# A four-layer graph network on one core: the s2 row sent round through memory, the layer-one slope on VectorE, the mask's diagonal in place, and a new order of the steps

## The reference, cut to what matters

```python
# layer 0
Wh = x @ W.T;  s1 = Wh @ a1;  s2 = Wh @ a2
e  = leaky_relu(s1[:, :, None] + s2[:, None, :], 0.2)
x  = layernorm(x + softmax(where(adj == 0, -inf, e)) @ Wh)
# layer 1
e  = leaky_relu(Ax.T + Ay + (h @ a_12) @ h.T, 0.2)
e  = where(adj > 0, e, -9e15)
x  = layernorm(x + elu(x @ W_1 + softmax(e) @ x @ W_2))
# layer 2: four heads, mask = adj | eye
x  = layernorm(x + relu(softmax(where(mask, q @ k.T * scale, min)) @ v @ Wo + bo))
# layer 3: relational convolution; with a 0/1 adj only relation 1 (the loop weights) is there
x  = layernorm(x + relu(onehot(adj.T == 1) @ ((h + b) * sigmoid(g + bg))))
```

## Time and profile before

| | |
|---|---|
| median of 3 runs | 497.16 us (495.63 to 498.61) |
| the profiled execution | 496.9 us, of which the span of the instructions is 495.0 us |
| mean granted TensorE clock | 0.988 of full speed |
| busy share PE, DVE, ACT, POOL | 95%, 83%, 86%, 75% |
| DMA | 26.93 MB, 54 GB/s in the mean |

### The profile page before, as it was taken

The page is one execution under the profiler, slowest core; times in us unless marked ns, Lnnn a source line. Parts: engine busy times, 40 slices in busy tenths (PEclk is TensorE's granted clock), DMA queues, the critical chain, the costliest instruction groups (busy, mean ns, idle before and its releaser), DMA issues. The chain is left out here.

```text
span 495.0 us, 13988 instructions
## 1 busy us (share of the span) xinstructions
PE 468.4 (95%) x3872; PEld 402.3 (81%) x3872; DVE 410.8 (83%) x1605; ACT 428.0 (86%) x1261; POOL 370.6 (75%) x736
## 2 busy tenths in 40 slices
PE   6968999999999999999999999999999999999793
PEld 5756778988888888988888888888888888877572
DVE  5657898998888998898888988898898989876653
ACT  3558999999999999999999999999999999988750
...
DMA packets 40222, 26.93 MB, mean 54 GB/s; under 512 B 2641, under 2 KB 39889, under 8 KB 40146
## 3 DMA queue, kind: packets, MB, share of 16 engines
...
...
## 5 line engine op out<-in xcount | busy, mean ns | idle before, releaser
L1211 POOL TENSOR_SCALAR x<-y,minus_mean,rstd 128x128 f32<-128x128 f32 x244 | 144.8, 601 | 6.8 <-issue 5.1
L788 ACT ACTIVATE p<-p,nmax 128x256 f32<-128x256 f32 x256 | 128.5, 530 | 0.4 <-DVE nmax L981 0.4
L981 DVE CUSTOM_DVE_ANT_0 p<-ps,neg 128x256 f32<-128x256 f32 x256 | 90.7, 420 | 2.3 <-PE ps L564 2.3
L1193 POOL TENSOR_TENSOR rstd<-ve,minus_half 128x2 f32<-128x2 f32 x128 | 91.1, 712 | 0.0
L575 PE MATMUL ps<-ident,p 128*128 128x128 f32 x512 | 78.0, 275 | 4.1 <-DVE nmax L981 3.4
L1186 POOL TENSOR_SCALAR ve<-stats 128x2 f32<-128x2 f32 x128 | 24.6, 192 | 72.3 <-DVE stats L896 64.9
L797 ACT COPY p2T<-ps 128x512 f32<-128x512 f32 x128 | 75.2, 590 | 1.3 <-PE ps L575 0.5
L575 PEld LDWEIGHTS ps<-ident,p 128*128 128x128 f32 x512 | 61.3, 143 | 9.3 <-DVE nmax L981 4.0
L788 ACT ACTIVATION_READ_ACCUMULATOR p<-p,nmax 128x1 f32 x256 | 56.1, 219 | 0.0
L896 DVE BATCH_NORM_STATS2 stats<-y 128x6 f32<-128x256 f32 x128 | 54.1, 423 | 1.5
L1175 POOL TENSOR_TENSOR relu<-relu,neg 128x512 f32<-128x512 f32 x32 | 37.1, 1161 | 21.1 <-ACT relu L757 21.1
(11 more groups left out here) (130 smaller groups left out, 1210.3 us busy)
## 6 DMA issues: line engine op xcount, KB each, us to landing
adj_in<-in_adj_dram SPq DMA_DIRECT2D x32, 256.0 KB, 3.0
xT<-in_xT_dram SPq DMA_DIRECT2D x32, 128.0 KB, 2.1
x_in<-in_x_dram SPq DMA_DIRECT2D x32, 128.0 KB, 2.1
x_aside<-x SPq DMA_DIRECT2D x32, 128.0 KB, 2.1
out_dram<-x SPq DMA_DIRECT2D x32, 128.0 KB, 2.9
...
l_w<-in_l_w_dram SPq DMA_DIRECT2D x1, 256.0 KB
...
```

What stands on the lines that cost most here:

```text
L788: last = nc.scalar.activation(p2(n)[:, k, a, :], p2(n)[:, k, a, :], ACT.Exp, bias=nmax2(n)[:, k, a:a + 1], scale=-1.0, accum_out=sum2(n)[: ...
L981: last = nc.vector.tensor_tensor_reduce(p2(n)[:, k, a, :], bank("sc2", n, a)[:, k * N:(k + 1) * N], neg2(n)[:, k, :], -1.0, HIGHEST, ALU.a ...
L1193: nc.gpsimd.tensor_tensor(rstd[layer](n), ve[layer](n), minus_half[:, :], ALU.pow)\
L1211: last = nc.gpsimd.tensor_scalar(dst[:, k, 0:D], y_t[layer](n)[:, k, :], minus_mean[layer](n)[:, k:k + 1], rstd[layer](n)[:, k:k + 1], ALU ...
```

## The change

- `first_w` gets a third column, so that `proj0` gives 0.8 s1, s2 and 0.2 s2 (131 columns per half).
- For graphs 3 to 31 `s2_rows` and `c_s2` are dropped. Instead SP writes the columns s2 and 0.2 s2 of `xw0` to memory (`s2_out`) and, once that has landed, reads them back as one row broadcast to all partitions (`s2_in`), into an `s2row` of 256 pairs. `e0` reads both of its operands from it, with a step of two elements. Graphs 0 to 2 go the old way.
- In layer 1 `relu1` becomes a copy scaled by 0.2, a new step `lk1` on DVE takes max(z, 0.2 z) over all 512 columns in one instruction, and `e1` reads its result and `neg1` from SBUF. `rmask1` on POOL is gone. The bank of `z1` is given back by `lk1`.
- `neg2` multiplies only the two 128 x 128 diagonal blocks of `neg0` in place, after `m0`; `e2a` and `e2b` read `neg0`, whose ring grows from 3 to 7, and `neg2`'s own ring is gone.
- Rings: `xw0` 3 to 4, `s2row` 2 to 3, `x4` 2 to 3. Two signals of the norm are merged into one semaphore.
- All places of `PLAN` are new; the flag steps go behind everything else.

```diff
 PLAN = {
-    "sync": [("ld_xT", 6707), ("ld_adj", 7906), ("ld_w", 8043), ("ld_x", 8602), ("aside", 16291), ("store", 19013)],
-    "tensor": [("proj0", 8774), ("s2_rows", 9402), ("prep_a", 11038), ("pT0", 11053), ("prep_c", 11151),
-        ("agg0", 11161), ("prep_d", 11846), ("prep_b", 12046), ("xT1", 12143), ("tT", 12198), ("z1", 12448),
-        ("xw1", 12450), ("pT1", 12863), ("flag", 13095), ("agg1", 13150), ("xT2", 13535), ("qk2", 13667),
-        ("sc2", 13818), ("pT2b0", 14335), ("pT2a0", 14520), ("pT2a1", 14582), ("rs_rows", 15014), ("v2", 15091),
-        ("pT2b1", 15180), ("agg2", 15365), ("wo2", 15578), ("xT3", 16401), ("hg3", 16731), ("agg3", 17296)],
...
+    "sync": [("ld_xT", 6855), ("s2_out", 8238), ("ld_adj", 8269), ("s2_in", 8279), ("ld_w", 8302), ("ld_x", 8425),
+        ("aside", 18831), ("store", 19788)],
+    "tensor": [("proj0", 7766), ("s2_rows", 8633), ("prep_a", 10144), ("pT0", 10921), ("agg0", 11174),
+        ("prep_c", 11246), ("prep_b", 11419), ("prep_d", 11635), ("xT1", 11809), ("tT", 11970), ("z1", 12536),
+        ("xw1", 12550), ("pT1", 12889), ("agg1", 13013), ("xT2", 13678), ("qk2", 13735), ("v2", 13789),
+        ("sc2", 13842), ("pT2b0", 14414), ("pT2a1", 14610), ("pT2a0", 14628), ("rs_rows", 15219), ("pT2b1", 15224),
+        ("agg2", 15554), ("wo2", 15760), ("xT3", 16986), ("hg3", 17357), ("agg3", 17727), ("flag", 18181)],
...
+    "vector": [("masks", 9909), ("e0", 10034), ("m0", 10553), ("s0", 11214), ("r0", 11237), ("y0", 11261),
+        ("b0", 11366), ("neg1", 11904), ("lk1", 12787), ("e1", 12887), ("eq1", 12923), ("r1", 13151), ("h1", 13179),
+        ("y1a", 13224), ("y1b", 13249), ("b1", 13250), ("e2b", 14078), ("e2a", 14095), ("r2", 14871),
+        ("onT2", 15861), ("y2a", 15925), ("y2b", 16347), ("b2", 16430), ("end_norm2", 16885), ("vals3", 17677),
+        ("y3", 17905), ("b3", 18072), ("end_norm3", 19319), ("flag_a", 27151), ("flag_b", 28488)],
+    "gpsimd": [("var0", 11715), ("rsq0", 11723), ("norm0", 11785), ("neg2", 11994), ("var1", 13438), ("rsq1", 13517),
+        ("norm1", 13518), ("rs_rep", 15026), ("var2", 16556), ("rsq2", 16866), ("norm2", 16947), ("var3", 18222),
+        ("rsq3", 19109), ("norm3", 19165)],
...
+            def s2_out(n):
+                sp.wait_ge(sem("wh_sb"), n + 1)
+                sp.dma_start(s2_dram[n].rearrange("(t p) c -> p t c", p=P), xw0(n)[:, :, 1:3])\
+                    .then_inc(sem(f"s2_out{n % 2}"), 16)
+
+            def s2_in(n):
+                sp.wait_ge(sem(f"s2_out{n % 2}"), 16 * ((n - PE_ROWS) // 2) + 16)
+                free(sp, "s2row", n, "e0_ready")
+                sp.dma_start(s2row(n).rearrange("p j c -> p (j c)"),
+                             s2_dram[n].rearrange("(a j) c -> a (j c)", a=1).broadcast_to((P, 2 * N)))\
+                    .then_inc(sem(f"s2_in{n % RING['s2row']}"), 16)
...
             def relu1(n):
-                nc.scalar.activation(relu(n).rearrange("p t n -> p (t n)"), bank("z1", n), ACT.Relu,
-                                     scale=(1.0 - SLOPE) / SLOPE).then_inc(sem("relu_ready"), 1)
+                nc.scalar.activation(relu(n).rearrange("p t n -> p (t n)"), bank("z1", n), ACT.Copy,
+                                     scale=SLOPE).then_inc(sem("relu_ready"), 1)
...
             def e0(n):
-                dve.wait_ge(sem("s2_sb"), n + 1)
+                if n < PE_ROWS:
+                    dve.wait_ge(sem("s2_sb"), n + 1)
+                    row = bank("s2_rows", n)[:, 0:N]
+                else:
+                    dve.wait_ge(sem(f"s2_in{n % RING['s2row']}"), 16 * ((n - PE_ROWS) // RING["s2row"]) + 16)
+                    row = s2row(n)[:, :, 0]
...
+                    last = nc.vector.scalar_tensor_tensor(out=p0(n)[:, k, :], in0=row, scalar=xw0(n)[:, k, 0:1],
+                                                          in1=s2row(n)[:, :, 1], op0=ALU.add, op1=ALU.max)
...
+            def lk1(n):
+                dve.wait_ge(sem("z_ps"), n + 1)
+                dve.wait_ge(sem("relu_ready"), n + 1)
+                o = bank("z1", n).rearrange("p (t n) -> p t n", t=T)
+                nc.vector.scalar_tensor_tensor(out=relu(n), in0=o, scalar=1.0, in1=relu(n), op0=ALU.mult, op1=ALU.max)\
+                    .then_inc(sem("leaky_ready"), 1)
...
             def e1(n):
-                dve.wait_ge(sem("rmask_ready"), n + 1)
+                dve.wait_ge(sem("leaky_ready"), n + 1)
+                dve.wait_ge(sem("neg1_ready"), n + 1)
                 free(dve, "p1", n, "pT_ps1")
-                o = bank("z1", n)
-                for k in range(T):
-                    last = nc.vector.tensor_tensor_reduce(p1(n)[:, k, :], o[:, k * N:(k + 1) * N], relu(n)[:, k, :],
-                                                          -SLOPE, HIGHEST, ALU.add, ALU.min, nmax1(n)[:, k:k + 1])
+                for k in range(T):
+                    last = nc.vector.tensor_tensor_reduce(p1(n)[:, k, :], relu(n)[:, k, :], neg1(n)[:, k, :],
+                                                          -1.0, HIGHEST, ALU.add, ALU.min, nmax1(n)[:, k:k + 1])
...
             def neg2_(n):
-                pool.wait_ge(sem("masks_ready"), n + 1)
-                free(pool, "neg2", n, "e2b_ready")
-                nc.gpsimd.tensor_tensor(neg2(n), neg0(n), not_eye[:, :, :], ALU.mult).then_inc(sem("neg2_ready"), 1)
-
-            def rmask1(n):
-                pool.wait_ge(sem("neg1_ready"), n + 1)
-                pool.wait_ge(sem("relu_ready"), n + 1)
-                nc.gpsimd.tensor_tensor(relu(n), relu(n), neg1(n), ALU.add).then_inc(sem("rmask_ready"), 1)
+                pool.wait_ge(sem("m0_ready"), n + 1)
+                nc.gpsimd.tensor_tensor(diagonal(n), diagonal(n), not_eye[:, :, :], ALU.mult).then_inc(sem("neg2_ready"), 1)
```

More of the change, by code:

```diff
@@ L66 @@
     **{step: (-1, 0) for step in ("flag_a", "flag", "flag_b")},
+    **{step: (0, PE_ROWS) for step in ("s2_rows", "c_s2")},
+    **{step: (PE_ROWS, 0) for step in ("s2_out", "s2_in")},
     **{step: (0, -AT_END) for step in ("norm2", "norm3")},
@@ L254, in build @@
         x3_dram = nc.dram_tensor("x3_aside", (B, P, T * D), F32, kind="Internal").ap()
+        s2_dram = nc.dram_tensor("s2_rows", (B, N, 2), F32, kind="Internal").ap()
         x_v = t["x"].rearrange("b (t p) d -> b p t d", p=P)
@@ L355, in _ @@
             sp.dma_start(first_w[:, :], t["first_w"]).then_inc(sem("w0_loaded"), 16)
-            run("sync", {"ld_adj": ld_adj, "ld_xT": ld_xT, "ld_x": ld_x, "ld_w": ld_w, "aside": aside, "store": store})
+            run("sync", {"ld_adj": ld_adj, "ld_xT": ld_xT, "ld_x": ld_x, "ld_w": ld_w, "s2_out": s2_out, "s2_in": s2_in, "aside": aside, "store": store})
             for s in range(RING["x4"]):
@@ L389, in setup @@
                 pe.wait_ge(sem("w0_loaded"), 16)
-                pe.matmul(ps[:, 0, 0:2], first_w[:, W0], first_w[:, 0:2], start=True, stop=True)\
+                pe.matmul(ps[:, 0, 0:3], first_w[:, W0], first_w[:, 0:3], start=True, stop=True)\
                     .then_inc(sem("setup_pe"), 1)
@@ L434, in flag @@
                 pe.wait_ge(sem("excess_ready"), 2)
-                pe.matmul(o[0:1, 0:1], excess[:, :], xw0_all[:, 0, 0, D + 2:D + 3], start=True, stop=True)\
+                pe.matmul(o[0:1, 0:1], excess[:, :], xw0_all[:, 0, 0, D + 3:D + 4], start=True, stop=True)\
                     .then_inc(sem("excess_ps"), 1)
@@ L473, in proj0 @@
                 for k in range(T):
-                    last = pe.matmul(o[:, k * (D + 2):(k + 1) * (D + 2)], xT0(n)[:, k * P:(k + 1) * P], w0_w[:, :],
+                    last = pe.matmul(o[:, k * (D + 3):(k + 1) * (D + 3)], xT0(n)[:, k * P:(k + 1) * P], w0_w[:, :],
                                      start=True, stop=True)
@@ L719, in c_s2 @@
                 free(act, "s2row", n, "e0_ready")
-                nc.scalar.mul(s2row(n), bank("s2_rows", n)[:, 0:N], SLOPE).then_inc(sem("s2_sb"), 1)
+                nc.scalar.mul(s2row(n)[:, :, 1], bank("s2_rows", n)[:, 0:N], SLOPE).then_inc(sem("s2_sb"), 1)
             def c_rs(n):
@@ L899, in e0 @@
             def e0(n):
-                dve.wait_ge(sem("s2_sb"), n + 1)
+                if n < PE_ROWS:
[4 more added lines that the diff above has]
+                    row = s2row(n)[:, :, 0]
                 free(dve, "p0", n, "pT_ps0")
                 for k in range(T):
-                    last = nc.vector.scalar_tensor_tensor(out=p0(n)[:, k, :], in0=bank("s2_rows", n)[:, 0:N],
-                                                              scalar=xw0(n)[:, k, 0:1], in1=s2row(n),
-                                                              op0=ALU.add, op1=ALU.max)
+                    last = nc.vector.scalar_tensor_tensor(out=p0(n)[:, k, :], in0=row, scalar=xw0(n)[:, k, 0:1],
+                                                          in1=s2row(n)[:, :, 1], op0=ALU.add, op1=ALU.max)
                 last.then_inc(sem("e0_ready"), 1)
@@ L981, in e2 @@
```

(11 more changed lines are left out.)

50 lines of the change are left out of this document (26 added, 24 removed), and 21 rows, old and new, of tables (PLAN, RING).

## The result

| | before | after |
|---|---|---|
| median of the runs of one session | 497.83 us (495.63 to 498.61, 4 runs) | 491.23 us (488.91 to 493.5, 4 runs) |
| the profiled execution, its span | 496.9, 495.0 us | 488.9, 487.1 us |
| ratio, with 95% interval | | 0.9875 (0.9839 to 0.991) |

The change makes the kernel 1.25% faster, 6.2 us by the ratio. The forecast was 491.0 us.

What follows compares the result with a forecast made beforehand. PE's own issue was taken to set the pace in the middle. From the profiled 496.9 us, -5.7 (middle), -1.3 (start) and +0.8 (end) gave 490.7; the median lies 0.3 higher, so 491.0 us, range 487 to 497.5.

Steps and rivals of the forecast that it cites:

- e0: DVE step, two a round, both operands now from SBUF: +0.07 us each, 0.14 in all, bounds -0.06 and 0.34.
- PE's round: One graph's worth of steps on PE in the middle: 14.00 - 0.22 + 0.01 = 13.79 us.
- the middle: The stretch where PE is always busy: 27 rounds, each shorter by 0.21 us, give 5.7 us.
- the sum: The prediction's addition of middle, start and end to 496.9 us, giving 490.7; its per-round costs feed into it.
- DVE's need: DVE work per round: 12.86 + 0.60 (lk1) + 0.06 (e1) + 0.14 (e0) = 13.66 us, 0.13 to spare.
- The shared port: Between DVE and POOL: two SBUF operands can cost up to 0.18 us; longer waits not borne out by the trace.
- Rival B: DVE becomes the bound through the port shared with POOL, needing 14.18 us a round: 501.6 us, chance 0.12.
- rival C: In-order waits of 0.1 to 0.3 us a round on DVE keep the round at 14.0: 496 us, chance 0.16.
- the prediction's own mark: DVE idle over 0.3 us a round, with short instructions, was to show that the in-order waits cost time.
- ACT and POOL: Work per round falls to 12.9 us on ACT and about 9.8 on POOL; neither can be the bound.
- The transfers: s2_out and s2_in: 5 us for both, 6 with issue and wait, bounds 3 and 12, all hidden.
- Start and end: Start booked at -1.3 us (bounds -4 and +2), end at +0.8 us (bounds 0 and +3).

Runs made afterwards that it cites:

- e4: The kernel before with only the s2 row of graphs 3 to 31 by transfers, s2row of 3 buffers, old order kept: 500.3 us, ratio 1.0068.
- e5: e4 with three places changed on DVE: e0 moved behind e2a, eq1 and neg1 into the gap it left: 503.6 us, ratio 1.0123.
- e8: The changed kernel with neg2 on POOL moved from 11994 to 11900, beside e0: 491.9 us (one run).
- e6: e4 with lk1 on DVE, which gives back z1's bank, and no rmask1 on POOL: 497.3 us, ratio 1.0003.
- e2: The changed kernel with layer one's slope and mask as before, on ACT and POOL (rmask1, no lk1): 516.9 us, ratio 1.0398.
- e7: The changed kernel with s2_rows (at 9762) and c_s2 (at 9845) for all graphs, no transfers of the s2 row: 502.3 us, ratio 1.0102.
- e9: The changed kernel with one more instruction of lk1's form on DVE in every round: 491.7 us, ratio 0.9897.
- e1: The changed kernel with s2_rows (at 9795) and c_s2 (at 9845) for all graphs, no transfers of the s2 row: 513.3 us, ratio 1.0313.
- e10: The changed kernel with two more instructions of lk1's form on DVE in every round: 495.2 us, ratio 0.9976.

## Why the prediction was right, point by point

**PE's round: right, its count with luck.** 13.79 forecast, 13.79 measured; the middle -5.7 forecast, -5.8 measured. The 27 rounds of the sum are 22 at full pace, worth 4.9 us; the other nine lost 0.9 us among them (between -0.62 and +0.59 each), for reasons that the sum doesn't have.

**DVE's need: the step that was mis-sized.** The prediction said 12.86 + 0.60 + 0.06 + 0.14 = 13.66 us; the round shows 12.82. `lk1` was sized well (685 ns for 670). `e0`'s pair lasts 0.87 us as before, not 0.14 more, and two `e1` take 0.04 less, not 0.06 more. What the sum left out is what the other instructions win: `y2b` from 562 to 417 ns, `neg1` from 505 to 429, `m0` from 454 to 416 (twice), `y1b` from 454 to 427, together 0.32 us in the mean, against 0.15 us more for `eq1` and its reduction. Two of the four pairs of norm statistics now follow each other directly and overlap (0.1 us). In 20 whole rounds DVE is busy for 12.60 us of a round before and 12.76 after: 0.15 us more, where the sum added 0.80. The small gaps between its instructions fell too, from 0.27 to 0.07 us. So DVE needs no more of a round than it did before. The instructions that won read SBUF and stood beside POOL's: I had read their spread as a cost that new instructions might have to pay, not as one that goes with POOL's work. That their gain is time in which POOL held the port is argued from e4, e5 and e8; no run shows it for each of them.

**The shared port: wrong, with no price here.** The sum took 454 ns as `m0`'s price for two SBUF operands, but that is a mean; the median of L913 is 421 ns, and `e1` came out at 401. The sentence that the trace bears out no wait of the length of a POOL instruction held for the trace of before alone: there the two long POOL instructions lie beside DVE instructions with an operand in PSUM (`rmask1` from 242.11 for 1.16 us beside `e0`, `neg2` from 247.80 beside `e2b`). e4, e5 and e8 show it cost up to 0.99, 0.87 and 0.4 us. Rival B did not come about for two reasons. The change takes `rmask1` away (e6 against e4), and in the new order `e0` would not have stood beside it: in e2, which has `rmask1` and the new order, the median of `e0` is 471 ns, with 998 as the longest.

**What hides what.** I costed the edits one by one and booked the gain to the dropped transposes. The runs show that it isn't theirs alone: e4 has them and is 0.7% slower; e6 has them and `lk1` and is where before was; with the order, and without `lk1`, the time is 516.9 (e2). `lk1` does three things: it ends DVE's wait for POOL, which the prediction had, it removes the long POOL instruction, which the prediction only weighed against B, and it frees `z1`'s bank early, which the prediction didn't have and which the new order needs.

**The in-order waits (rival C): half there.** `y1b` still waits, 0.28 us for 0.53, and two waits are new, 0.35 and 0.33 us. By the prediction's own mark (over 0.3 us a round) C should have cost time. It did not, since DVE had 1 us and not 0.13. The mark was badly chosen: the two new waits are DVE's for PE, and an engine with time to spare waits for the one that paces the round.

**ACT and POOL.** ACT: 253.07 / 20 = 12.65 us, forecast 12.9. POOL: 210.78 / 20 = 10.5, forecast 9.8; `neg2` cost 0.67 for 0.6, and the reciprocal root rose from 712 to 815 ns, four times a round. Both hidden, as forecast.

**The transfers: right that they are hidden, off in size.** 4.2 + 3.5 = 7.7 us for both, forecast 6 with the issue and within its bounds; SP's wait 83.6 / 29 = 2.9 us, forecast 2 to 3. Not forecast: `ld_adj` takes 5.3 us to land instead of 3.0; in the middle nobody waited for it. It takes 3.1 us with the transfers in the old order (e4) and 2.7 in the new order without them (e7), so it is its place right behind `s2_out` on SP.

**Start and end: neither measured what was booked.** Forecast -1.3 and +0.8, measured -0.5 and -1.6. The start varies more than it was booked: `sc2(0)` stands at 38.7 us in after and at 41.4 and 42.3 in e8 and e9, whose steps up to there are nearly the same ones in the same order. PE's first difference is a load: all three have the same start at 7.88 us, and then `proj0` of graph 2 waits for its `xT` for 0.38, 0.89 and 1.57 us:

```profile
8.95 1.21 PE L495 MATMUL ps<-first_w,xT 128*128 128x131 f32 x4 [0.38 <-DMA xT<-in_xT_dram]
10.14 1.21 PE L495 MATMUL ps<-first_w,xT 128*128 128x131 f32 x4 [1.57 <-DMA xT<-in_xT_dram]
```

Behind that the granted clock falls too: from 20 to 30 us it is 1.00 in after, 0.87 in e8 and 0.92 in e9. How the 2.7 and 3.6 us divide between the two stays open.

The end goes with the granted clock, and not with the order. The last 25 us of after, of e4 (the old order) and of e7 (the new one), against the earlier trace rows:

```profile
462.10:487.10 25.00, 14.88 (x118) 11.32 (x118) 13.33 (x44) 9.13 (x29) 10.78 (x27) 0.91 0.17 48
472.40:497.40 25.00, 14.52 (x116) 11.01 (x116) 12.16 (x38) 9.34 (x29) 7.86 (x21) 0.90 0.15 43
474.20:499.20 25.00, 15.71 (x114) 11.47 (x113) 11.90 (x36) 7.70 (x22) 10.77 (x27) 0.84 0.17 49
```

At 0.90 and more the end takes 28.4 us in after, e2, e8 and e9 and 28.2 in e4; at 0.84 it takes 29.6 to 30.0 in before, e1, e5, e6, e7 and e10. So the 1.6 us belong to a clock that after's profiled execution got and before's did not, and the deeper order costs nothing at the end, where the sum booked 0.8. Without them 6.3 of the 7.9 us between the two spans are left, which is what the medians say. The flag steps lay beside the last store, as forecast. Against the profiled execution the sum is 1.8 us too high: the end gives -2.4 of it, the start +0.8, the middle -0.1.

The time was right because the bound was: PE paced the round, and DVE's error had the harmless sign. With half the error the other way, 0.4 us more on DVE, it would have needed 14.1 us of a round, and the time would have come near rival B's (an estimate from the sum). That the forecast lies within 0.3 us of the median is luck: the rounds in which the pipeline fills and empties made up for five that the sum counted too many, and the errors of start (0.8 too low) and end (0.8 too high, the clock left aside) cancelled.
